# A mixture of experts in seven-product form: one down product moved forward within each chunk pair

## What is computed

```python
g = jnp.einsum('bsd,edf->ebsf', h, Wg)
u = jnp.einsum('bsd,edf->ebsf', h, Wu)
expert_outs = jnp.einsum('ebsf,efd->ebsd', jax.nn.silu(g) * u, Wd)
expert_output = jnp.einsum('be,ebsd->bsd', gating_probs, expert_outs)
shared = jnp.einsum('bsf,fd->bsd', jax.nn.silu(h @ Sg) * (h @ Su), Sd)
x = x + (1.0 - sg) * expert_output + sg * shared
```

## Time and profile before

| | us |
|---|---|
| median of 3 runs | 2124.58 (2123.74 to 2124.72) |
| the profiled execution | 2123.92 |
| its span | 2122.1 |
| PE busy | 2098.0 (99%), 9180 matmuls |
| PEld busy | 1717.0 (81%) |
| DVE busy | 1452.6 (68%) |
| ACT busy | 1303.7 (61%) |
| POOL busy | 1609.4 (76%) |

### The profile page before, as it was taken

The page is one execution under the profiler, slowest core; times in us unless marked ns, Lnnn a source line. Parts: engine busy times, 40 slices in busy tenths (PEclk is TensorE's granted clock), DMA queues, the critical chain, the costliest instruction groups (busy, mean ns, idle before and its releaser), DMA issues.

```text
span 2122.1 us, 33959 instructions
## 1 busy us (share of the span) xinstructions
PE 2098.0 (99%) x9180; PEld 1717.0 (81%) x9180; DVE 1452.6 (68%) x2640; ACT 1303.7 (61%) x2336; POOL 1609.4 (76%) x1435
## 2 busy tenths in 40 slices
PE   7999999999999999999999999999999999999998
PEld 5888888888788888888878888888887888888886
DVE  6666666666666666666676666666667666666666
ACT  6777777777556555555555655555555555555554
POOL 7988777878388777777778877777777777777776
PEclk9999999999999999999999999999999999999999
DMA  8776767666555455455445555445445555544543
GB/s 297 243 250 224 253 225 249 227 241 225 191 208 208 177 206 199 173 198 208 176 188 204 189 200 207 177 187 208 189 177 206 185 201 206 202 173 196 208 180 117
DMA packets 122455, 433.78 MB, mean 204 GB/s; under 512 B 13728, under 2 KB 41504, under 8 KB 122400
## 3 DMA queue, kind: packets, MB, share of 16 engines
q1 hardware_dynamic: 122400, 433.19, 54.5%
HBM read 329.85 MB, written 103.28 MB: 204 GB/s over the span
## 4 chain that ended last, share of the span: by engine, by line
PE 97%; DVE 1%; issue 0%; DMA 0%; POOL 0%; ACT 0%; SPq 0%; DVEq 0%; ACTq 0%; POOLq 0%
PE chain_ps L549 15%; PE chain_ps L551 14%; PE chain_ps L550 14%; PE down_ps L551 8%; PE down_ps L549 8%; PE down_ps L550 8%; PE p_ps L549 6%; PE p_ps L551 6%; PE p_ps L550 6%; PE side_ps L549 4%; PE side_ps L550 4%; PE side_ps L551 4%; DVE acc L972 1%; DMA w_raw<-w 0%; DVE h_forms L975 0%
## 5 line engine op out<-in xcount | busy, mean ns | idle before, releaser
L386 POOL TENSOR_TENSOR h_forms<-h_t,h_forms 128x512 fp32r<-128x512 f32 x432 | 564.3, 1325 | 274.2 <-ACT h_forms L858 274.2
L549 PE MATMUL chain_ps<-x_hi,gate_forms 128*128 128x512 f32 x1080 | 423.9, 393 | 2.2 <-DVE p_ps L972 1.1
L551 PE MATMUL chain_ps<-x_hi,gate_forms 128*128 128x512 f32 x1080 | 421.1, 390 | 0.0
L550 PE MATMUL chain_ps<-x_lo,gate_forms 128*128 128x512 f32 x1080 | 420.8, 390 | 0.0
L386 POOL TENSOR_TENSOR h_t<-h_b,h_t 128x512 f32<-128x512 f32 x214 | 312.6, 1461 | 78.9 <-DVE h_b L966 63.6
L972 DVE TENSOR_TENSOR p_ps<-tap_p,chain_ps 128x512 f32<-128x512 f32 x216 | 150.3, 696 | 251.5 <-PE chain_ps L551 251.5
L875 ACT COPY chain_ps<-chain_ps 128x512 f32<-128x512 f32 x216 | 123.1, 570 | 289.3 <-DVE h_a L966 201.3
L858 ACT CAST h_forms<-h_t 128x512 fp32r<-128x512 f32 x432 | 268.9, 623 | 14.9 <-DVE h_t L975 2.2
L386 POOL TENSOR_TENSOR w_lo<-w_raw,w_hi 128x1152 fp32r<-128x1152 f32 x71 | 190.5, 2683 | 85.7 <-ACT w_hi L775 84.8
L549 PEld LDWEIGHTS chain_ps<-x_hi,gate_forms 128*128 128x128 f32 x1080 | 202.5, 188 | 60.9 <-ACT chain_ps L875 8.1
L551 PEld LDWEIGHTS chain_ps<-x_hi,gate_forms 128*128 128x128 f32 x1080 | 202.7, 188 | 43.4
(11 more groups left out here) (105 smaller groups left out, 4882.2 us busy)
## 6 DMA issues: line engine op xcount, KB each, us to landing
gate_forms<-kept_gate SPq DMA_DIRECT2D x216, 896.0 KB, 7.4
down_forms<-kept_down SPq DMA_DIRECT2D x108, 896.0 KB, 4.6
kept_gate<-w_hi SPq DMA_DIRECT2D x72, 448.0 KB, 2.5
kept_gate<-w_lo SPq DMA_DIRECT2D x72, 448.0 KB, 3.0
w_raw<-w SPq DMA_DIRECT2D x72, 256.0 KB, 3.2
w_raw<-w SPq DMA_DIRECT2D x72, 128.0 KB, 2.9
kept_down<-d_hi SPq DMA_DIRECT2D x36, 256.0 KB, 2.9
kept_down<-d_lo SPq DMA_DIRECT2D x36, 256.0 KB, 2.9
```

Source lines behind the costliest of these rows:

```text
L386: return nc.gpsimd.tensor_tensor(dst, a, b, ALU.subtract)
L549: nc.tensor.matmul(bank, w_high, hi, start=start, stop=False, **on)
L550: nc.tensor.matmul(bank, w_high, lo, start=False, stop=False, **on)
L551: return nc.tensor.matmul(bank, w_low, hi, start=False, stop=stop, **on)
```

## The change

q3 of the pair before moves from slot 20 to slot 14, between q4 and p6(nb). p6, p2, q7, p7, p3 of the second chunk and q2 each stand one slot later; the body still ends after 21 products. The final addition of q3's bank moves on DVE from the end of a group's second body to the end of its first. SP's fetch waits for q2, which is now the last q product of a body.

```diff
@@ fetch (SP)
-                    sp.wait_ge(q_done[3], pair(g, e, k // 2) - 1)
+                    sp.wait_ge(q_done[2], pair(g, e, k // 2) - 1)
                     fetch_down(e, k // 2)
@@ two_groups (PE)
                 p5(nb, kb)
                 down_step(4, 0, CHUNKS - 1, 1)
+                down_step(3, None, None, None)
                 p6(nb, kb)
                 p2(kb)
                 down_step(7, None, None, None)
                 p7(nb, kb)
                 p3(kb)
                 down_step(2, None, None, None)
-                down_step(3, None, None, None)
@@ two_groups (DVE)
                     tap(7, gp, pc - 1, is_first(ep, jp))
                 else:
                     add(1)
+                if first and g > 1:
+                    finish_q(3, gp, [acc[:, 2 * gp + 1, 0, :]])
                 if second and g > 1:
                     finish_q(2, g - 1, [acc[:, 2 * (g - 1), 0, :]])
-                    finish_q(3, g - 1, [acc[:, 2 * (g - 1) + 1, 0, :]])
```

## The result

The changed kernel is slower: the median is 2149.28 us (2148.95 to 2149.87, 5 runs) against 2124.58 us (2123.37 to 2126.68, 5 runs) for the kernel before. The ratio is 1.0117, with a 95% interval of 1.0107 to 1.0128. The medians differ by 24.7 us; 20.0 were forecast, and the time lies inside the range. The span of the profiled execution grew from 2122.1 to 2147.5 us, by 25.4 us.

The account below looks back on a forecast made before the run. PE's matmuls and waits were taken to bound the kernel. 23.5 + 0.6 + 0.7 - 4.8 = +20.0 us on 2123.92 gave 2143.9, and 0.7 more for the runs' median 2144.6 us; range 2130 to 2153.

Parts of the forecast that it names:

- The bound: Whole kernel: time is PE's 9180 matmuls plus PE's waits; PE busy 2098.0 of 2122.1 us, 97% of the chain.
- The gain at p6: p6(nb) at slot 14: standing one product, 0.68 us, later, it no longer waits for ACT's seed; -4.8 us.
- The chain to p4: From q7 over three DVE steps to the next p4: 2.37 us, load 0.10 us late, 0.23 us 102 times, +23.5 us.
- the rival in which weights are fetched ahead of it: At p4: only the load's lateness, 0.10 us, is paid 102 times; sum +6.5 us, 2131 us; chance 6%.
- h1 and POOL: At p5, slot 2, and POOL's first subtraction: both move later but make PE wait no longer; 0 us.
- The group boundaries: Bodies 36, 37, 72, 73: p4 of 37 and 73 costs +0.83 each, 37 and 73 shrink 0.6 and 0.5; +0.6 us.
- bodies 37 and 73 should be shorter than before: Sign expected in the changed profile: these two bodies, 16.27 and 15.49 us before, get shorter.
- The end: Last products: q6 waits behind a chain from the last p3, which ends one product later; +0.7 us.
- p4 in time: Rival at p4: the three DVE steps shorten by 0.2 us, so the new wait vanishes; 2120.5 us; chance 7%.
- A second link: Rival: later h1 or POOL makes p5, q6 or q4 late too, +15 us, 2160 us; chance 10%.
- The clock: Rival: short idles in every body lower TensorE's clock; one body in ten at half speed over 150 us; chance 1%.

Follow-up runs that it names:

- Experiment 3: The changed kernel with q3 one product later, behind p6 of the second chunk instead of ahead of it: 2152.72 us, ratio 1.0136.
- experiment 1: The changed kernel with up1 ahead of the low part of B11 in DVE's queue: 2192.14 us, ratio 1.0324.
- experiment 2: The changed kernel with DVE's low part of B11 and up1 moved ahead of the tap of q7: 2147.73 us, ratio 1.0112.
- Experiment 5: The changed kernel with q3's final addition behind the low part of B11 in DVE's queue, still ahead of up1: 2147.97 us, ratio 1.0115.
- experiment 4: The kernel before with one more DVE copy from PSUM between q7's tap and the low part of B11, in 107 bodies: 2247.78 us, ratio 1.0581.
- kernel 9: The changed kernel with B11 made early, q3's final addition behind the second body's up1(na), and POOL's token sum behind low T1: 2121.80 us, ratio 0.999.
- kernel 8: The changed kernel with B11 early, its low part behind u4(nb) in 22 bodies, q3's final addition behind the second body's up1(na): 2124.78 us, ratio 1.0007.

## Why the prediction was right or wrong

**The bound: right.** PE is 97% of the chain before and after, the clock stayed at its level of 2.4 GHz (granted 1.000), and every us of the difference is a wait of PE.

**The gain at p6: right.** Forecast 4.8 us. Of the 38 waits for the seed, 34 stood at p6(nb), and all of these went. Slots 14 to 17 held 48 ns a body; 5 ns are left at p6's new place and behind it, so the gain is 4.4 us over 102. Experiment 3 brings the 38 waits back, with 3.1 us of span. The count of 38 says less than it seems: the trace of before has p6's load late against a free one in all 99 ordinary bodies, by 0.16 to 0.19 us in 34 and by 0.06 or 0.07 us in 65, and the profile lists only the longer waits. After, none is late.

**The chain to p4: right.** Its 2.37 us came out as 2.37 us, in the same three steps, and the load was 0.10 us late. The gap behind it was 0.109 us wider (forecast 0.105). The starts further behind took 0.04 us instead of 0.025, so one p4 costs 0.25 and not 0.23 us: 25.4 us instead of 23.5 (0.4 us of it falls into bodies 36, 72 and 107). Experiments 1 and 2 show that the wait is DVE's queue. The wait itself is dearer than its lateness, as body 38 of before had said, and the rival in which weights are fetched ahead of it, at 2131 us, fell with it.

**h1 and POOL: right for the change, and only just.** The load of p5 at slot 2 is never late (the 11 ns there are the unevenness behind p4), and PE waits for POOL no more than before. But experiment 1, with h1 0.8 us later still, shows how near the second link stood.

**The group boundaries: the term that was mis-sized.** The forecast had +0.6 us; measured was +4.06. Bodies 36 and 72 grew by 1.81 and 1.80 us where +0.83 each was forecast; body 37 shrank by 0.12 instead of 0.6, and body 73 grew by 0.58 instead of shrinking by 0.5. The failed step is "Two additions took 1.27 us, one holds the queue 0.60 us. p4 of bodies 37 and 73 is late by 0.70 us". The addition does hold the queue 0.60 us, but what it pushes back is not only later, it is longer. The low part of B11 reads two tiles of SBUF, and so does POOL's low part of T1. Whichever starts first has its way: DVE first, 0.68 us and POOL 1.42 (body 22 after); POOL first, DVE 1.65 us and POOL 1.29 (body 36 after). In the trace of before DVE was first, by 0.40 us in body 22 (882.48 against the row below), and I never asked what would become of it with that lead gone. Experiment 5 gives back just this part by the order of two steps, and experiment 4 makes it in every body of the kernel before.

```profile
882.88 1.44 POOL L386 TENSOR_TENSOR h_forms<-h_t,h_forms 128x512 fp32r<-128x512 f32 x1 [2.74 <-ACT h_forms L858]
```

In body 73 it is the same step with a twist: there an addition *less* does the harm. The timelines at the end of body 73, DVE and POOL, first of the kernel before, then of the changed one:

```profile
1616.78 1.28 POOL L386 TENSOR_TENSOR h_forms<-h_t,h_forms 128x512 fp32r<-128x512 f32 x1 [2.71 <-ACT h_forms L858]
...
1618.14 0.68 DVE L975 TENSOR_TENSOR h_forms<-h_a,h_forms 128x512 fp32r<-128x512 f32 x1
```

```profile
1634.27 0.68 DVE L972 TENSOR_TENSOR acc<-down_ps,acc 128x512 f32<-128x512 f32 x1
1634.68 1.28 POOL L386 TENSOR_TENSOR h_forms<-h_t,h_forms 128x512 fp32r<-128x512 f32 x1 [3.35 <-ACT h_forms L858]
1634.87 1.64 DVE L975 TENSOR_TENSOR h_forms<-h_a,h_forms 128x512 fp32r<-128x512 f32 x1
```

Before, the additions of q2 and q3 held the low part of B11 until POOL was done (1616.78 and 1.28 make 1618.06; it starts at 1618.14). Now q2's stands alone, the low part starts 0.19 us behind POOL's start, and all that q3's absence saved, and more, is lost: p4 of body 74 comes 1.30 us late. The forecast had counted on 0.60 us less of DVE's queue there. The tell "bodies 37 and 73 should be shorter than before" was right for 37 (16.15 against 16.27 us) and wrong for 73 (16.07 against 15.49).

Body 37 gave back 0.12 us and not 0.6, for a like reason. Its p7 waits for `u4`, `u4` stands in DVE's queue behind the two additions of `u3_sum`, and these took 3.20 us in the changed kernel:

```profile
1102.89 3.20 DVE L972 TENSOR_TENSOR acc<-u_sum,acc 128x512 f32<-128x512 f32 x2
```

In the trace of before the same pair took 2.86 us. So p7 waited 0.79 us where I had 0.39; 0.34 of that 0.40 is the pair's growth. No run varied this pair alone; the shorter 2.33 us in kernel 9 and the longer 3.41 in kernel 8 go with where POOL's steps stand.

The Trainium skill has this mechanism, in "SBUF — State Buffer", section "Who interferes with whom": a DVE instruction with two SBUF inputs contends with a GpSimd instruction that reads SBUF, and "Issue order, not op shape, decides who blocks." The traces agree: the blocked step ends 0.54 us after POOL's (1092.40 to 1092.94), and `up1` and the taps, which read PSUM, keep 0.68 and 0.69 us beside a running POOL. Put into the sum, two times 0.97 us makes the forecast +21.9, body 73's 1.1 and body 37's 0.5 make it +23.5, and the 1.8 of the ordinary bodies +25.3, beside +25.4 in the spans.

**The end: right.** 0.85 us instead of 0.7 from body 107 on, 0.25 of it in body 107 itself, whose closing p4 the forecast had not counted.

**The rivals.** p4 in time: false, the three steps kept their lengths and starts. A second link: not in the change, but it is what experiments 1 and 2 run into. The clock: no. Of the range, the upper side was used: 4.7 us of mis-sizing, with 8.4 allowed.

## What to carry to other kernels

When a product is moved forward past others, whoever stood behind it loses its cover: count, on the in-order engine that feeds the next consumer, the queue from the last late input to that consumer, and compare it with the matmuls that are left. When a step on DVE with two SBUF inputs is shifted, look also at which POOL steps run beside it, before and after the shift: the step's length hangs on which of them is first. And where reordering the queue only hands the wait to the next consumer (experiments 1 and 2), take out of the queue a step whose input is ready much earlier.

## What the runs showed of the hardware

- A DVE addition or subtraction of 128x512 with two SBUF inputs took 0.68 us alone or when it started first, and 1.57 to 1.68 us when it started 0.15 to 0.26 us behind a POOL step of 1.29 us. In the bodies quoted the blocked step ended 0.54 to 0.55 us after POOL's. POOL's step took 1.41 to 1.44 us when DVE was first by 0.4 us. The low part of B22 stands beside POOL's first subtraction: it started 0.06 us before that one ended in body 23 of before, and 0.52 us before it ended in the same body after. It went from 0.70 us on the mean before to 1.08 us after, at no cost to PE. The group below holds it together with the low part of B21, which also reads `h_b` and stayed at 0.69 us; the group's mean was 0.695 us before:

```profile
L975 DVE TENSOR_TENSOR h_forms<-h_b,h_forms 128x512 fp32r<-128x512 f32 x214 | 189.3, 884 | 0.0
```

(The changed kernel's groups of instructions by line and shape: count, then busy us and mean ns of one.) 214 times 0.189 us is 40 of the 44.7 us by which DVE's busy time grew.

- A weight load that waits costs more than it is behind its matmul's due time, and something already when it is just ahead of it. With the load 0.10 us behind its matmul's due time a p4 cost 0.25 us (the changed kernel), and with it about 0.04 us ahead of the due time 0.106 us (experiment 2). With the load late against its usual start by 0.16 to 0.19 us, 0.07 to 0.04 us ahead of the due time, a seeded product cost 0.06 to 0.09 us (34 bodies of before). With it 0.11 us ahead of the due time, p5 of experiment 2 lost nothing that shows. Each figure is the lateness and some unevenness of the starts behind it.

- Some 104 short idles of TensorE, one in each body, left the granted clock at 1.000.
